# Neighbour tables of a graph kernel padded to two rounds a tile, with a loop for chunks of two rounds

## What is computed

```
q, k, v = heads(h @ Wq + bq) * scaling, heads(h @ Wk + bk), heads(h @ Wv + bv)
s = einsum('edh,edh->eh', q[rows], k[cols])
e = exp(s - segment_max(s, rows)[rows]);  attn = e / segment_sum(e, rows)[rows]
out = segment_sum(attn[:, None, :] * v[cols], rows) @ Wo + bo      # pass "att": rows=src, cols=dst

h = (h_in @ W).reshape(n, 4, 64)                                    # passes "gt0" and "gt1"
e = leaky_relu(alpha_s[src] + alpha_d[dst], 0.2)
alpha = softmax of e over the edges of one dst
out = segment_sum(h[src] * alpha[:, :, None], dst) + b;  gelu
```

## Time and profile before

| | |
|---|---|
| timed runs | 4384.58 us median of 3 (4378.15 to 4388.7) |
| the profiled execution | 4348.89 us, span 4347.2 us |
| busy share of the span | PE 61%, PEld 43%, DVE 53%, ACT 34%, POOL 44% |
| gathers of neighbours (L925) | 480 in `att`, 960 in `gt0` and `gt1` |
| stages in the profiled execution | tables to 930 us, `att` 1078 to 1831 us, `gt0` 2591 to 3300 us, `gt1` 3393 to 4126 us |

### The profile page before, as it was taken

How to read it: one execution, slowest core, us unless ns; L and a number is a source line. 1 busy time by engine, 2 the same in 40 slices (tenths; PEclk the granted TensorE clock), 3 DMA queues, 4 the chain that set the end, 5 groups by cost and what they waited for, 6 DMA issues and landing times. The chain is left out here.

```text
span 4347.2 us, 64875 instructions
## 1 busy us (share of the span) xinstructions
PE 2658.8 (61%) x14881; PEld 1883.4 (43%) x14882; DVE 2313.9 (53%) x6656; ACT 1486.1 (34%) x4433; POOL 1910.7 (44%) x1935
## 2 busy tenths in 40 slices
PE   7688858846355555445999744445545445545479
PEld 4552456214233333334999723333334233333368
DVE  8679966964577777644111234444445344444442
ACT  0359325941567676510444310001002100000044
POOL 1010011021677777540222356767664666666611
PEclk9789669978666677665999856667677666677689
DMA  0640056023666666522122123333332333333300
GB/s 10 166 106 0 3 124 148 0 98 113 160 183 174 182 182 180 139 67 66 55 93 75 53 82 88 93 87 91 89 90 63 87 92 89 87 89 90 81 27 18
DMA packets 259389, 404.17 MB, mean 93 GB/s; under 512 B 99719, under 2 KB 181173, under 8 KB 259197
## 3 DMA queue, kind: packets, MB, share of 16 engines
q0 software_dynamic: 101040, 302.00, 26.3%
q1 hardware_dynamic: 156416, 99.57, 9.2%
q10 hardware_dynamic: 1872, 1.85, 0.1%
HBM read 366.39 MB, written 36.88 MB: 93 GB/s over the span
## 5 line engine op out<-in xcount | busy, mean ns | idle before, releaser
L925 POOL DMA_INDIRECT gt_rows<-h_rows,gt_idx x960 | 1001.9, 1044 | 460.2 <-issue 296.2
L1105 PE MATMUL gt_part<-gt_wv,all_ident 128*128 128x260 f32 x1920 | 709.0, 536 | 780.3 <-DVE gt_wv L1008 435.6
L1105 PEld LDWEIGHTS gt_part<-gt_wv,all_ident 128*128 128x128 f32 x1920 | 491.4, 267 | 997.9 <-DVE gt_wv L1008 497.2
L1105 PE MATMUL att_part<-att_wv,all_ident 128*128 128x264 f32 x960 | 374.4, 559 | 398.3 <-remote 136.3
L925 POOL DMA_INDIRECT att_rows<-kv_rows,att_idx x480 | 519.1, 1081 | 195.7 <-issue 194.5
L1082 ACT ACTIVATE gt_wv<-gt_score 128x20 f32<-128x20 f32 x240 | 57.1, 238 | 1327.9 <-issue 694.9
L1105 PEld LDWEIGHTS att_part<-att_wv,all_ident 128*128 128x128 f32 x960 | 252.6, 276 | 520.3 <-issue 383.7
L1087 ACT ACTIVATE att_wv<-att_rows,att_wv 128x32 f32<-128x32 f32 x1920 | 428.4, 308 | 109.3 <-remote 55.6
L1008 DVE TENSOR_TENSOR gt_wv<-gt_rows,gt_wv 128x1024 f32<-128x1024 f32 x240 | 292.6, 1219 | 0.4 <-ACT gt_wv L1082 0.4
L1022 DVE TENSOR_TENSOR gt_acc<-gt_acc,gt_part 128x260 f32 x240 | 102.0, 425 | 241.6 <-remote 105.9
L1450 PE MATMUL ex_up<-ex_xe,ex_w 128*128 128x128 f32 x1760 | 208.5, 277 | 11.6 <-DVE ex_xe L1414 11.6
(11 more groups left out here) (466 smaller groups left out, 5226.0 us busy)
## 6 DMA issues: line engine op xcount, KB each, us to landing
ex_w<-in_W SPq DMA_DIRECT2D x16, 1024.0 KB, 7.6
gt_rows<-h_rows,gt_idx POOLq DMA_INDIRECT x960
ixbs_parts_bc<-key_parts_s SPq DMA_DIRECT2D x14, 1024.0 KB
ixbs_parts_bc<-key_parts_s SPq DMA_DIRECT2D x28, 512.0 KB, 6.8
ixbd_parts_bc<-key_parts_d SPq DMA_DIRECT2D x14, 1024.0 KB
ixbd_parts_bc<-key_parts_d SPq DMA_DIRECT2D x28, 512.0 KB, 6.9
att_rows<-kv_rows,att_idx POOLq DMA_INDIRECT x480
y_rows<-ex_y POOLq DMA_DIRECT2D x55, 128.0 KB, 2.0
```

What stands on the lines that cost most here:

```text
L925: pool.indirect_dma_start(out=rows[:, k, r, :], out_offset=None, in_=table, in_offset=bass.IndirectOffsetOnAxis(ap=idx[:, k, r:r + 1], axi ...
L1105: last = pe.matmul(part[:, k, 0:h * av], c.ident[:, :], wv[:, k, r, :, :].rearrange("p h f -> p (h f)"), start=(r == 0), stop=(r == ROUNDS ...
```

## The change

The table is laid out with each tile's rounds rounded up to pairs. A tile with an odd number of pairs ends in a *tail* of two rounds. Chunks of four rounds are numbered first (`full` of them), the tails behind them; both counts go through `counts`. Since the place of a chunk no longer follows from its number, `tile_of` gets a second row with the first column of each chunk. For this `ahead` grows to 25 x 2 x (104 + 32) numbers a lane, with two more products, and the tails' part of the list is written by a second DMA behind the first. In `attend` every engine has a second loop behind the first, over blocks of four tails, in which each chunk has two gathers, two products on PE and half the elements on DVE and ACT. SP reads the column of each chunk from the list before it loads the indices. `neighbours` is one array of 53248 columns a lane in place of windows, and `zeros` is bf16. The core of the diff, without unchanged lines:

```diff
@@ -13,6 +13,7 @@
...
+TAIL_ROUNDS = ROUNDS // 2
@@ -20,9 +21,14 @@
...
-MAX_CHUNKS = (N_EDGES + 3 * NT + 4 * NT) // ROUNDS + 1
-MAX_WIN = -(-MAX_CHUNKS * ROUNDS // WIN)
-MAX_CHUNKS = MAX_WIN * WIN // ROUNDS
+SLOTS = 4
+TAIL = 32
+SPARE = ROUNDS * (SLOTS - 1)
+MAX_WIN = -(-(N_EDGES + 3 * NT + SPARE) // WIN)
+MAX_COLS = MAX_WIN * WIN
+MAX_CHUNKS = MAX_COLS // ROUNDS
+MIN_FULL = (N_EDGES // P - 3 * NT) // ROUNDS
+MAX_FULL = MAX_CHUNKS - TAIL - SLOTS
@@ -301,21 +308,26 @@
...
-                    step(dve.tensor_scalar(ch_f[:, :], mdeg[:, :], float(ROUNDS - 1), float(ROUNDS), ALU.add, ALU.max))
-                    step(dve.tensor_copy(ch_i[:, :], ch_f[:, :]))
-                    step(dve.tensor_single_scalar(ch_i[:, :], ch_i[:, :], 2, ALU.logical_shift_right))
-                    step(dve.tensor_copy(ch_f[:, :], ch_i[:, :]))
-                    step(dve.memset(cum[:, 0:1], 0.0))
-                    step(dve.tensor_tensor_scan(cum[:, 1:NT + 1], c.ones[:, 0:NT], ch_f[:, :], 0.0, ALU.mult, ALU.add))
-                    step(dve.tensor_copy(g.first_chunk[:, :], cum[:, :]))
+                    step(dve.tensor_scalar(rounds_i[:, 3, :], mdeg[:, :], 1.0, 2.0, ALU.add, ALU.max))
+                    step(dve.tensor_single_scalar(rounds_i[:, 0, :], rounds_i[:, 3, :], 1, ALU.logical_shift_right))
+                    step(dve.tensor_copy(within[:, :], rounds_i[:, 0, :]))
+                    step(dve.memset(cum[:, :, 0:1], 0.0))
...
-                                           cum[:, 0:NT].unsqueeze(1).to_broadcast([P, NT, NT]), ALU.mult))
+                                           cum[:, 0, 0:NT].unsqueeze(1).to_broadcast([P, NT, NT]), ALU.mult))
...
-                    step(dve.tensor_scalar(base_of[:, :], base_of[:, :], float(ROUNDS), None, ALU.mult))
+                    step(dve.tensor_scalar(base_of[:, :], base_of[:, :], 2.0, None, ALU.mult))
...
+                    step(dve.tensor_single_scalar(rounds_i[:, 1, :], rounds_i[:, 0, :], 1, ALU.logical_shift_right))
+                    step(dve.tensor_single_scalar(rounds_i[:, 2, :], rounds_i[:, 0, :], 1, ALU.bitwise_and))
+                    step(dve.tensor_copy(rounds_f[:, :, :], rounds_i[:, 1:3, :]))
+                    for k in (1, 2):
+                        step(dve.tensor_tensor_scan(cum[:, k, 1:NT + 1], c.ones[:, 0:NT], rounds_f[:, k - 1, :], 0.0, ALU.mult, ALU.add))
+                    step(dve.tensor_copy(g.counts[:, 0:1], cum[:, 1, NT:NT + 1]))
+                    step(dve.tensor_scalar(g.counts[:, 1:2], cum[:, 2, NT:NT + 1], 1.0, None, ALU.max))
@@ -544,8 +556,9 @@
...
-            chunk_f, tile_f, tile_i = d.sb("chunk_f", [P, CPL]), d.sb("tile_f", [P, CPL]), d.sb("tile_i", [P, CPL], I32)
-            ahead = d.sb("ahead", [P, NT, CPL])
+            LISTED = CPL + TAIL
+            chunk_f, tile_f, tile_i = d.sb("chunk_f", [P, CPL]), d.sb("tile_f", [P, 2, LISTED]), d.sb("tile_i", [P, 2, LISTED], I32)
+            ahead = d.sb("ahead", [P, NT, 2, LISTED])
@@ -578,30 +591,47 @@
...
-                    dve.wait_ge(counted, 8)
-                    dve.tensor_scalar(tile_f[:, :], tile_f[:, :], 0.5, NT / 2, ALU.mult, ALU.add).then_inc(tiled, 1)
-                    dve.wait_ge(tiled, 1)
-                    dve.tensor_scalar(tile_f[:, :], tile_f[:, :], float(NT - 1), None, ALU.min).then_inc(tiled, 1)
-                    dve.wait_ge(tiled, 2)
-                    dve.tensor_copy(tile_i[:, :], tile_f[:, :]).then_inc(tiled, 1)
+                    dve.wait_ge(counted, 13)
+                    tile, col = tile_f[:, 0, :], tile_f[:, 1, :]
+                    dve.tensor_scalar(tile, tile, 0.5, NT / 2, ALU.mult, ALU.add).then_inc(tiled, 1)
+                    dve.scalar_tensor_tensor(col[:, 0:CPL], chunk_f[:, :], float(ROUNDS), col[:, 0:CPL], ALU.mult, ALU.add).then_inc(tiled, 1)
+                    dve.tensor_tensor(col[:, CPL:LISTED], col[:, CPL:LISTED], c.iota_f[:, 0:TAIL], ALU.add).then_inc(tiled, 1)
+                    dve.wait_ge(tiled, 3)
+                    dve.tensor_scalar(tile_i[:, 0, :], tile, float(NT - 1), None, ALU.min).then_inc(tiled, 1)
+                    dve.tensor_tensor(tile_i[:, 1, 0:CPL], col[:, 0:CPL], cum[:, 2, NT:NT + 1].to_broadcast([P, CPL]), ALU.add).then_inc(tiled, 1)
+                    dve.tensor_tensor(col[:, CPL:LISTED], col[:, CPL:LISTED], cum[:, 1, NT:NT + 1].to_broadcast([P, TAIL]), ALU.add).then_inc(tiled, 1)
+                    dve.wait_ge(tiled, 6)
+                    dve.tensor_scalar(tile_i[:, 1, CPL:LISTED], col[:, CPL:LISTED], 2.0, None, ALU.mult).then_inc(tiled, 1)
...
+                    def past(out, at, of):
+                        n = out.shape[-1]
+                        pool.tensor_tensor(out, at.unsqueeze(1).to_broadcast([P, NT, n]), of.unsqueeze(2).to_broadcast([P, NT, n]), ALU.subtract).then_inc(counted, 1)
...
+                    def counting(row, of):
+                        n = row.shape[-1]
+                        pool.tensor_tensor(row, row, of.unsqueeze(2).to_broadcast([P, NT, n]), ALU.mult).then_inc(counted, 1)
...
-                    pool.tensor_tensor(ahead[:, :, :], chunk_f[:, :].unsqueeze(1).to_broadcast([P, NT, CPL]),
-                                       cum[:, 1:NT + 1].unsqueeze(2).to_broadcast([P, NT, CPL]), ALU.subtract).then_inc(counted, 1)
+                    for r in range(2):
+                        past(ahead[:, :, r, 0:CPL], chunk_f[:, :], cum[:, 1, 1:NT + 1])
+                        past(ahead[:, :, r, CPL:LISTED], c.iota_f[:, 0:TAIL], cum[:, 2, 1 - r:NT + 1 - r])
...
+                    counting(ahead[:, :, 1, 0:CPL], rounds_f[:, 1, :])
+                    counting(ahead[:, :, 1, CPL:LISTED], rounds_f[:, 0, :])
+                    pool.wait_ge(counted, 7)
...
-                        pool.tensor_tensor(ahead[:, 0:n, :], ahead[:, 0:n, :], ahead[:, other:other + n, :], ALU.add).then_inc(counted, 1)
-                        pool.wait_ge(counted, k + 3)
-                    pool.tensor_tensor(tile_f[:, :], ahead[:, 0, :], ahead[:, NT - 1, :], ALU.add).then_inc(counted, 1)
+                        pool.tensor_tensor(ahead[:, 0:n, :, :], ahead[:, 0:n, :, :], ahead[:, other:other + n, :, :], ALU.add).then_inc(counted, 1)
+                        pool.wait_ge(counted, k + 8)
+                    pool.tensor_tensor(tile_f[:, :, :], ahead[:, 0, :, :], ahead[:, NT - 1, :, :], ALU.add).then_inc(counted, 1)
...
-                    act.wait_ge(counted, 2)
-                    act.activation(ahead[:, :, :], ahead[:, :, :], ACT.Sign, bias=c.ones[:, 0:1], scale=2.0).then_inc(signed, 1)
+                    act.wait_ge(counted, 5)
+                    act.activation(ahead[:, :, :, :], ahead[:, :, :, :], ACT.Sign, bias=c.ones[:, 0:1], scale=2.0).then_inc(signed, 1)
@@ -637,12 +667,15 @@
...
-                        sp.dma_start(g.neighbours[bass.ds(w, 1), :, :].rearrange("a p c -> (a p) c"), table_i[:, :]).then_inc(stored, 16)
-                    sp.wait_ge(tiled, 3)
-                    sp.dma_start(g.tile_of.rearrange("(p n) -> p n", p=P), tile_i[:, :]).then_inc(tiles_out, 16)
+                        sp.dma_start(g.neighbours[:, bass.ds(w * WIN, WIN)], table_i[:, :]).then_inc(stored, 16)
+                    sp.wait_ge(tiled, 7)
+                    sp.dma_start(g.tile_of.rearrange("r (p n) -> p r n", p=P), tile_i[:, :, 0:CPL]).then_inc(tiles_out, 16)
+                    full = sp.value_load(g.counts[0:1, 0:1], min_val=MIN_FULL, max_val=MAX_FULL)
+                    sp.wait_ge(tiles_out, 16)
+                    sp.dma_start(g.tile_of[:, bass.ds((full + (SLOTS - 1)) // SLOTS * SLOTS, TAIL)].unsqueeze(0), tile_i[0:1, :, CPL:LISTED]).then_inc(tiles_out, 16)
...
-                    sp.wait_ge(tiles_out, 16)
+                    sp.wait_ge(tiles_out, 32)
@@ -879,31 +910,42 @@
...
-            total = eng.value_load(g.first_chunk[0:1, NT:NT + 1], min_val=NT, max_val=MAX_CHUNKS)
-            return eng.snap((total + (SLOTS - 1)) // SLOTS)
+            full = eng.value_load(g.counts[0:1, 0:1], min_val=MIN_FULL, max_val=MAX_FULL)
+            tails = eng.value_load(g.counts[0:1, 1:2], min_val=1, max_val=NT)
+            full = eng.snap((full + (SLOTS - 1)) // SLOTS)
+            return full, eng.snap(full + (tails + (SLOTS - 1)) // SLOTS)
...
-                def load_idx(j, k):
...
-                    sp.dma_start(idx[:, k, :], g.neighbours[bass.ds(j // (WIN // ROUNDS), 1), :, bass.ds((j % (WIN // ROUNDS)) * ROUNDS, ROUNDS)]
-                                 .rearrange("a p c -> (a p) c")).then_inc(idx_in[k], 16)
+                def load_idx(col, k):
...
+                    sp.dma_start(idx[:, k, :], g.neighbours[:, bass.ds(col, ROUNDS)]).then_inc(idx_in[k], 16)
...
+                def col_of(j):
+                    return sp.value_load(tile_of[1:2, bass.ds(j, 1)], min_val=0, max_val=MAX_COLS - ROUNDS)
...
-                    load_idx(k, k)
-                sp.dma_start(tile_of[:, :], g.tile_of.rearrange("(a n) -> a n", a=1)).then_inc(tiles_in, 16)
```

(41 more changed lines are left out.)

101 lines of the change are left out of this document (57 added, 44 removed).

## The result

| | before | after |
|---|---|---|
| timed runs, median | 4383.61 us (6 runs, 4373.07 to 4392.84) | 4331.93 us (6 runs, 4325.43 to 4345.2) |
| profiled execution | 4348.89 us | 4338.7 us |

The ratio is 0.9888, with a 95% interval of 0.9869 to 0.9906. By the medians the kernel is 52 us faster (41 to 57 by the interval), where the prediction had 14. The two profiled executions differ by 10 us only. That discrepancy, 10 against 52, had to be settled before any term could be judged.

A forecast was written before the change was run, and what follows sets the result against it. POOL's issue of gathers was taken as the bound, DVE close behind. Terms of -85 (passes), +57 (table builder), +6 (second loops) and +8 (SP) gave -14 us, from the timed median 4384.6 to 4371 us; range 4325 to 4425.

The forecast's parts named there:

- Gathers removed: In attend: 24 gathers fewer a pass, 72 in all, 456 a pass, with the number of chunks staying 120.
- The gain in the passes: In the three attend passes: 26.6 us in `att`, 55.1 in `gt`, 3 in the drain, together 85 us (46 to 116).
- The tail blocks: Last three blocks of each attend pass: 15 us each, ends 13.4 and 18 in `att`, 10.8 and 20 in `gt`.
- The drain: Work behind the last gather of each pass, on two rounds too: about 1 us a pass saved, 3 us.
- The reads by SP and the second loops: Added in attend: 8 us for SP's column reads, 2 us a pass or 6 us for one more loop per engine.
- The table builder: Longer list around the window loop: 28.4 us added per graph, 57 for both, ends 40 and 61.
- the held DVE: Window loop: POOL's adds block DVE's L572, costing 13.8 us more per graph; the low end was 5.8.
- The base: Starting time: profiled execution of 4348.9 us, 36 us below the timed median of 4384.6, for which the forecast was made.
- full blocks changed their pace: One of the signs named as proving the forecast wrong; full blocks of attend were to keep their pace.
- The full saving: Rival 1: no DVE stop in the tails, POOL's adds cost in proportion; gain 115, cost 44, -71 us, 4314; chance 0.22.
- The slow sequencers: Rival 2: more SP instructions make slow stretches of SP and DVE more frequent, +85 us, sum +63, 4448 us; chance 0.25.
- That the change keeps 480 gathers: Rival 3: padding by slots keeps 480 gathers, only costs are left, +71 us, 4456 us; chance 0.03.

The follow-up runs named there:

- e9: After with tiles rounded up to four rounds again, so all costs and no savings: 4474.37 us, ratio to before 1.0219.
- e5: The kernel after, unchanged, timed again beside before: 4329.1 us, ratio 0.9889.
- e8: The kernel before, unchanged, profiled once more: one execution of 4370.55 us, no ratio.
- e10: The kernel before, unchanged, profiled yet again: one execution of 4372.46 us, no ratio.
- e6: Before, with SP also waiting for the list and reading each chunk's tile from it in attend: 4381.45 us, ratio to before 1.0018.
- e3: After, with the list of tiles and columns cut to 256 chunks: 4007.42 us, ratio 0.9733 to before at 4121.1 us.
- e7: After, with the list made by DVE ahead of the window loop instead of on POOL and ACT: 4289.25 us, ratio to before 0.9788.
- e1: The kernel before, unchanged, timed against itself where before takes 4121.1 us: 4118.28 us, ratio 0.9995.

## Why the prediction was right and where its sizes were off

**Right in sign, and the range held the time,** but -14 us was measured as -52.

**Gathers removed: right.** 24 a pass, 72 in all, with 120 chunks as before.

**The gain in the passes: the step that was mis-sized.** It was put at 85 us. The runs give two measures. By the times it is 52 + 62 = 114 us (62 the costs from e9). By the windows and drains of the profiles (means of after and e5 against e8 and e10) it is 28, 32 and 22 us in the three passes and 9.5 us in the drains: 92. Two terms of the sum were mis-sized:
- The tail blocks, taken at 15 us, took 14.3 and 14.1 us in `att` and 12.4 to 14.1 in `gt`. I had put 4 us of DVE's stops into every `gt` tail block. But the stops fall into some blocks and not into others: by the starts of the gathers the three tail blocks of after's first `gt` pass took 17.0, 11.6 and 11.1 us. Six `gt` blocks at the mean of 13.4 give 10 us more, three `att` blocks at 14.2 another 2.
- The drain, taken at 1 us a pass, is 5.3 us shorter in `att` (12.5 against 17.8) and 0.5 and 3.7 us in `gt`: 6.5 us more.

The pace of the blocks saved, 24.2 and 24.3 us in e8 and e10 where I had 23.85 and 24.19, adds 2. That makes 85 + 12 + 6.5 + 2 = 105. So the gain that was put at 85 is 105 by its own terms; the profiles' 92 are this less 13 us, by which the 78 full blocks come out longer than in e8 and e10.

**The reads by SP and the second loops: 8 and 6 us put down.** e6 measured 5.5 us (1 to 15) for the first, without tail blocks. The second was not isolated.

**The table builder: right, term by term.** Per graph, after against before: POOL's and ACT's part ahead of the loop 17.9 against 7.0 us, +10.9 (predicted 11.4); the loop 193.3 against 178.9 us, +14.4 (predicted 13.8); from ACT's last tile to the next stage's first DMA 7.0 against 4.3 us, +2.7 (predicted 2.9). The 0.3 us for the chain ahead of it can't be seen: POOL's first subtraction starts at 285.2 and 280.1 us in after and e5, at 285.5, 283.0 and 283.1 in the first profile, e8 and e10. The sum is 28 a graph, 56 in all, predicted 57 (of the stated ends the terms give 41 for the low one of 40; for the high one of 61 no working is shown, and the upper end of the gain, 116, adds up to 115). A second reading agrees: the first gather of `att` starts at 1069.9 to 1077.9 us in the six profiles with the old builder and at 1124.2 to 1134.1 in the four with the new one, 56 us apart in the mean. e9's 62 us for all additions would be these 56 and e6's 5.5, with nothing left for the second loops, but the interval of e9 is too wide to tell. The choice between 13.8 and 5.8 for the held DVE fell as the rows said: L585 took 7.11 us beside an add of 7.05. The loop of e3, with POOL's work short, takes before's 178.8 us, and that of e7, with it gone, 176.5. The rule cited from the Trainium skill, page "SBUF — State Buffer", section "Who interferes with whom", that of VectorE in a two-port mode and GpSimd the one that issues first holds the shared ports for its whole instruction and the other is blocked, agrees with this row and with these loops.

**The base: wrong, though it cost little here.** I noted that the profiled execution was 36 us below the timed runs, and carried its rows over unchanged. It was not typical: e8 and e10 lie 22 and 24 us above it in their own time. Taken by itself this moves the sum by the 2 us above, nine full blocks at 0.2 to 0.35. But it misled the reading of the result: profile against profile, the full blocks seem to have become 0.5 us slower, 40 us in all, and this is the "full blocks changed their pace" that the prediction had named as what would make it wrong. e6, e8 and e10 show that most of it is scatter between executions (or between chips: the first profile's isn't on record).

**What stays open.** The two measures of the gain, 92 and 114 us, aren't brought together. With the intervals of the two timings the second is 98 to 131 us, so the 105 of the terms lies within it and the profiles' 92 just below. The profiled executions of before (4349 to 4372 us) all lie below the median of its timed runs (4382 to 4385), and so does e1's (4111 against 4118); those of after (4339 and 4329) don't; where these some 10 us sit in a timed run no profile shows. How much of the 13 us of longer full blocks is e6's 5.5 and how much scatter isn't told apart either.

**The rivals.** The full saving (-71 us, 4314) is nearer to the result than its chance of 0.22 said: its gain of 115 is what the times give with e9, but its cost of 44 was 62, mostly since DVE was held for the whole of each add. That its gain fits is chance: its `gt` tails of 10.8 us took 13.4, its `att` tails of 13.4 took 14.2, and the drain, which it took at 3 us, gave 9.5. The slow sequencers at their full price are excluded by e6. That the change keeps 480 gathers is excluded by the count of 456. One argument in the prediction was misread: that POOL waited for DVE only 0.6 us in `att`, so that most `att` blocks run without a stop. The earlier trace rows has 194.5 us of "issue" before 480 gathers, where 0.30 us each would be 144; the other 50 are stops without a named releaser. So `att` had stops as well, and the first of its tail blocks took 16.4 us in after and 15.4 in e5.

## What to carry to other kernels

Price a held engine by the whole time of the instructions that hold it: here the loop grew by 14.4 us a graph for some 15 us more of POOL's work beside it. Take small list work away from beside a loop that is paced by DVE: the longer list cost 56 us on POOL and ACT, and the kernel that makes it on DVE ahead of the loop is 40 us faster. Don't read "issue" as "no stop": compare it with the count times the usual pause. Take a second profile of the kernel before where the first lies outside its timed runs, since rows that differ by 2% between executions look like an effect of the change. Where a term can't be separated, build the kernel with all costs and no savings: e9 split a difference of 52 us into some 114 gained and 62 lost, each to within 10 to 15 us.

## What the runs showed of the hardware

The same program takes 4121 us in one group of runs, 4343 in another and 4376 to 4385 in the rest. Of the 259 us between the spans of e1 and e8, 219 lie in the three passes of `attend` (71, 83 and 65 us by the windows above). In the slower case single sequencer instructions of SP and DVE take 0.70 us in place of 0.03 to 0.2, in stretches of some 20 us that come about every 50 us in `gt`; on POOL, ACT and PE the traces hold hardly any (2, 0 and 0 in e10). ACT is slowed in another form: its activations at L1087 start 1.4 us apart in stretches, 31 and 27 times in e8 and e10, once in e1. TensorE's mean granted clock differs little, 0.782 against 0.769, and the gathers themselves take 1.05 us on both. What sets the slow stretches off, and why they are missing in one group, isn't known from these runs; chip number 9 has runs of both kinds. A case like this one has two answers, then: what a saved block is worth (21.7 or 24.3 us), and whether 3 more instructions a chunk on SP cost 0 or 5 us, depends on whether the stretches are there.
